# A pre-norm attention block and a feed-forward block in one kernel: the order of work changed at the start, at the change of batch, at the entrance of the feed-forward part and over its last product

## What is computed

```python
def attn(x, Wqkv, bqkv, Wo, bo):                    # one head, d = 256
    q, k, v = split(x @ Wqkv + bqkv, 3)
    a = softmax(q @ k.T / 16)
    return (a @ v) @ Wo + bo

def ffn(h, gate_w, up_w, down_w, fc1_w, fc2_w, expert_w, gamma, beta):
    top = sum(top_k(h @ gate_w, 2))                 # per row
    shared = relu(h @ up_w)**2 @ down_w             # 1024 -> 2048 -> 1024
    routed = ((h @ fc1_w) @ expert_w * top) @ fc2_w # 1024 -> 512 -> 512 -> 1024
    return norm(shared + routed) * gamma + beta

x = x + attn(norm(x), ...)
x = x + ffn(norm(x), ...)
```

## Time and profile before

| what | us |
|---|---|
| median of 3 runs | 2403.39 |
| lowest and highest of them | 2400.56, 2404.26 |
| the profiled execution's own time | 2403.08 |
| its span in the trace | 2401.2 |
| PE busy | 2320.8 (97% of the span) |
| DVE busy | 1748.3 (73%) |
| POOL busy | 1565.5 (65%) |
| ACT busy | 907.8 (38%) |

### The profile page before, as it was taken

How to read it: one execution, slowest core, us unless ns; L and a number is a source line. 1 busy time by engine, 2 the same in 40 slices (tenths; PEclk the granted TensorE clock), 3 DMA queues, 4 the chain that set the end, 5 groups by cost and what they waited for, 6 DMA issues and landing times.

```text
span 2401.2 us, 31321 instructions
## 1 busy us (share of the span) xinstructions
PE 2320.8 (97%) x11224; PEld 1937.2 (81%) x11224; DVE 1748.3 (73%) x2946; ACT 907.8 (38%) x1707; POOL 1565.5 (65%) x1180
## 2 busy tenths in 40 slices
PE   7999999999999899999999999999999999999996
PEld 5888889888988788878877887887787787788875
DVE  5889857876887544854689865479785368977868
ACT  4222233432434343444433443432344343344442
POOL 4466535664666776599557489846659974844584
PEclk8999999999999999999999999999999999999998
DMA  8899847778778633435345343535444533533452
GB/s 232 263 305 301 252 140 196 216 218 283 218 200 230 209 113 95 130 90 149 97 140 163 101 127 94 151 94 172 130 115 105 138 109 109 185 106 97 119 158 88
DMA packets 216090, 386.48 MB, mean 161 GB/s; under 512 B 19584, under 2 KB 95488, under 8 KB 215296
## 3 DMA queue, kind: packets, MB, share of 16 engines
q1 hardware_dynamic: 214784, 382.38, 54.1%
q10 hardware_dynamic: 1152, 2.10, 0.2%
HBM read 260.67 MB, written 90.18 MB: 146 GB/s over the span
## 4 chain that ended last, share of the span: by engine, by line
PE 55%; DVE 18%; POOL 13%; DMA 6%; issue 5%; SPq 2%; ACT 1%; DVEq 0%; POOLq 0%; ACTq 0%
PE ps L2199 18%; PE ps L2201 18%; PE ps L2200 18%; DVE pturn L1334 5%; POOL hq L2041 4%; DMA pland<-pturn 4%; POOL wr1l L1957 2%; POOL wr0l L1957 2%; POOL wr2l L1957 2%; SPq L638 1%; DVE x L1361 1%; DVE mx L1317 1%; DVE xi L1270 1%; DVE xr L1599 1%; DVE st L1368 1%
## 5 line engine op out<-in xcount | busy, mean ns | idle before, releaser
L1957 POOL TENSOR_TENSOR wr2l<-stf,wr2h 128x512 fp32r<-128x512 f32 x183 | 261.0, 1426 | 153.3 <-ACT wr2h L963 153.2
L1957 POOL TENSOR_TENSOR wr0l<-stf,wr0h 128x512 fp32r<-128x512 f32 x184 | 258.5, 1405 | 150.5 <-ACT wr0h L963 150.2
L1957 POOL TENSOR_TENSOR wr1l<-stf,wr1h 128x512 fp32r<-128x512 f32 x183 | 256.6, 1402 | 152.2 <-ACT wr1h L963 152.2
L963 ACT CAST wr1h<-stf 128x512 fp32r<-128x512 f32 x183 | 113.8, 622 | 310.1 <-PE ps L2201 268.4
L963 ACT CAST wr0h<-stf 128x512 fp32r<-128x512 f32 x184 | 114.5, 622 | 307.6 <-PE ps L2201 270.3
L963 ACT CAST wr2h<-stf 128x512 fp32r<-128x512 f32 x183 | 113.9, 622 | 303.6 <-PE ps L2201 255.8
L1957 POOL TENSOR_TENSOR pt<-pland,pt 128x512 fp32r<-128x512 f32 x120 | 153.0, 1311 | 69.6 <-ACT pt L942 69.6
L932 ACT ACTIVATE prob<-ps,nm 128x512 f32<-128x512 f32 x128 | 86.3, 688 | 251.7 <-DVE nm L1325 251.7
L1334 DVE STREAM_TRANSPOSE pturn<-prob 128x512 f32<-128x512 f32 x128 | 131.9, 1094 | 56.5 <-DMA pland<-pturn 51.1
L1212 DVE TENSOR_TENSOR hr1l<-hq,hr1h 128x512 fp32r<-128x512 f32 x78 | 98.2, 1259 | 85.4 <-ACT hr1h L986 85.1
L1212 DVE TENSOR_TENSOR hr0l<-hq,hr0h 128x512 fp32r<-128x512 f32 x78 | 91.5, 1173 | 89.5 <-ACT hr0h L986 89.5
(11 more groups left out here) (488 smaller groups left out, 7774.0 us busy)
## 6 DMA issues: line engine op xcount, KB each, us to landing
stf<-ups SPq DMA_DIRECT2D x160, 256.0 KB, 3.0
stf<-downs SPq DMA_DIRECT2D x160, 256.0 KB, 2.9
pland<-pturn SPq DMA_DIRECT2D x120, 256.0 KB, 4.7
stf<-in_upw_dram SPq DMA_DIRECT2D x120, 256.0 KB, 2.6
stf<-in_down_dram SPq DMA_DIRECT2D x88, 256.0 KB, 2.6
x<-in_x_dram SPq DMA_DIRECT2D x32, 512.0 KB, 6.5
x1d<-x SPq DMA_DIRECT2D x32, 512.0 KB, 5.6
xi<-in_x_dram SPq DMA_DIRECT2D x28, 512.0 KB, 9.4
```

The costliest lines, as they stand in the source:

```text
L963: eng.copy(hi, src).then_inc(*a_w.up(K))
L1957: eng.tensor_tensor(lo, src, hi.bitcast(F32), ALU.subtract).then_inc(*done)
```

## The change

**Start.** Three more stage buffers, and a table STG_BUF that says which piece goes into which. Two low parts (et 2, f2 2/0) go from DVE to POOL, et 3 from POOL to DVE behind the root, one piece (f2 2/1) is taken ahead of the variance. DVE norms 5 of 16 groups, not 4. ACT takes one more piece ahead of the norm, and interleaves E2's first two banks with the first two slab pieces.

**Change of batch.** In pair 7 DVE takes the turns of group 15 ahead of the moments of units 2 and 3 and of the root; SP issues group 15's shuffle and the key loads ahead of `store1(5)` and `qload(9)`; POOL's `norm2(5)` goes behind the split of group 14. In pair 8 `xadd(7)` goes first on POOL and `at_hi`/`at_low`(7,1) go earlier. In pair 9 PE runs output unit 0 of pair 7 ahead of the scores, not behind.

**Entrance of the feed-forward part.** POOL splits weights 0, 1 and 2 ahead of `xadd(15)` and `norm2(14)`.

**Last half block.** The order of the products becomes 1, 2, 6, 5, 3, 7, 4. The last product runs wholly by banks: all ten steps for bank 0, then for bank 1, 2, 3. Its weights and hidden rows are prepared earlier, with other buffers. The x rows of tiles 0 to 3 are loaded and beta added in the up half (steps 46 to 59), those of tiles 4 to 7 at down steps 0 to 11. Tiles 0 to 3 are finished during the last product, tiles 4 and 5, then 6 and 7, behind it, all on DVE.

The core of the diff:

```diff
-DOWN = [(1, 2, 6, 3, 7, 4, 5)] * 3 + [(1, 2, 6, 7, 4, 5, 3)]
+DOWN = [(1, 2, 6, 3, 7, 4, 5)] * 3 + [(1, 2, 6, 5, 3, 7, 4)]
...
-    late = [47, 48, 49, 51, 53, 54, 55, 57, 58, 59]
+    late = [38, 40, 42, 47, 48, 49, 50, 51, 57, 58]
...
+        STG_BUF = [0, 1, 2, 3, 4, 0, 1, 2, 3, 4, 0, 5, 6, 7, 1, 2, 3]
-        STG_DVE = [("et", 0), ("f2", 0, 0), ("f2", 0, 1), ("f2", 1, 1), ("et", 2), ("f2", 2, 0), ("f2", 2, 1)]
+        STG_DVE = [("et", 0), ("f2", 0, 0), ("f2", 0, 1), ("f2", 1, 1), ("f2", 2, 1), ("et", 3)]
...
-        for i, s in enumerate((41, 43, 45, 47, 49, 51, 53, 58, 59, 60)):
+        for i, s in enumerate((31, 33, 35, 37, 39, 41, 43, 45, 47, 49)):
... SyncE, attention
+                if C == 7:
+                    xload(C - 1)
+                    shuffle(odd)
+                    for kb in (2, 3):
+                        load_k(kb)
                 if C >= 2:
                     store1(C - 2)
-                xload(C - 1)
+                if C != 7:
+                    xload(C - 1)
...
-                if C < 15:
+                if C < 15 and C != 7:
                     shuffle(odd)
-                if C == 7:
-                    for kb in (2, 3):
-                        load_k(kb)
... SyncE, last block, up half
+                        if fin and s in (46, 48, 50, 52):
...
+                            load_x1(n, t, xrl[t])
... ScalarE, start
-            for k in STG[:11]:
+            for k in STG[:12]:
                 stage_hi(k)
...
-            for k in STG[11:13]:
-                stage_hi(k)
-            for j in range(2):
-                slab_hi(0, j)
+            stage_hi(STG[12])
+            slab_hi(0, 0)
+            e2_evac(0)
+            slab_hi(0, 1)
+            e2_evac(1)
             for k in STG[13:15]:
                 stage_hi(k)
-            for lt in range(2):
-                e2_evac(lt)
... VectorE, start
             aggr1(0, stats1(0, 8, 16), 8, 16)
+            low(stg_parts(("f2", 2, 1)), a_stg["f2", 2, 1], v_stg.up(("f2", 2, 1)))
             diff1(0)
-            for k in STG_DVE[4:]:
-                low(stg_parts(k), a_stg[k], v_stg.up(k))
             rstd1(0)
...
+            low(stg_parts(("et", 3)), a_stg["et", 3], v_stg.up(("et", 3)))
... VectorE, pair 7
                     for u in (2, 3):
                         residual(C - 2, u)
+                    turns(odd)
+                    at_low(C - 1, 0)
+                    for u in (2, 3):
                         moments(C - 2, u)
+                    at_low(C - 1, 1)
                     ln2(C - 2, *range(15))
-                    at_low(C - 1, 0)
-                    turns(odd)
-                    at_low(C - 1, 1)
... GpSimd, entrance and up half of the last block
-            w_low(0)
+            for k in range(3):
+                w_low(k)
             xadd(15)
             norm2(14, 0)
             norm2(14, 1)
-            w_low(1)
-            w_low(2)
...
+                        if fin and s in (50, 53, 56, 59):
+                            add_beta(n, (s - 50) // 3, xrl[(s - 50) // 3])
... TensorE
+                elif C == 9:
+                    wo_unit(C - 2, 0)
+                    scores(even)
+                    wo_unit(C - 2, 2)
+                    wo_unit(C - 2, 3)
...
-            for ts in ((0, 1), (2,), (3,)):
-                for s in range(63, 70):
-                    down_mm(NBK - 1, s, ts)
+            for t in range(4):
+                for s in range(60, 70):
+                    down_mm(NBK - 1, s, (t,))
```

More of the change, by code:

```diff
@@ L840, in _ @@
                             load_x1(n - 1, t + 2, xr[t % 2])
[L841 to L843 removed]
+                for s in range(60 if fin else 70):
+                    turnover(PER * n + 70 + s)
                     if not fin:
```

338 lines of the change are left out of this document (139 added, 199 removed).

## The result

| | us |
|---|---|
| before, median of 4 runs | 2403.23 (2400.56 to 2404.26) |
| changed, median of 4 runs | 2389.91 (2388.09 to 2395.01) |
| changed against before | 0.995, 95% interval 0.9931 to 0.9968 |
| forecast | 2378.0, range 2371 to 2388 |

A forecast was written before the change was run, and what follows sets the result against it. PE was busy 97%, so time could come only from its gaps, half-clock stretches and the work after its last matmul; -4.2 -0.6 -4.8 +0.5 -6.4 -9.5 = -25.0 against 2403.08 gave 2378, range 2371 to 2388.

The forecast's parts named there:

- Start, -4.2: Start: first projection 2.75 us earlier and its half-clock stretch gone, 1.45; bounds -1.5 and -6.
- Change of batch, -0.6: Pairs 7 to 9: wait at 538 goes, but store1(5) lands behind the keys and delays pv(7,0); bounds +1.5 and -3.5.
- Rival A: Change of batch: stores land with or before the keys, pv(7,0) about 3 us earlier, sum 2374; chance 0.15.
- Entrance, -4.8: Feed-forward entrance: 5.73 wait and 1.6 at half clock go, part given back, step 4 at 807.45; bounds -2.5 and -6.5.
- Last block, up half, +0.5: Last block's up half: eight beta additions on POOL cost little, using DVE's idle time; bounds 0 and +5.
- rival B: Up half: POOL's additions hold DVE, PE waits 2.8 and loses 1.7 or more; 5 us, 2382.5; chance 0.16.
- My worst case: Up half: all eight additions delay DVE in full, 10.4 us against 5.6 caught up; wait 2.8, stretch 1.7 or more.
- Down half, -6.4: Last block's down half: waits and 3.05 of half clock go, 7.2, less 0.8 at steps 49 and 50; bounds -3.5 and -7.2.
- End, -9.5: Behind PE's last matmul: only the last bank's work is left, 11.8 to 12.0 us for 21.5; bounds -7 and -10.5.
- Rival C: End: DVE comes late, its spare of 3 being an estimate; end gains only 5, sum 2382.7; chance 0.13.
- Rival D: Last product: PE starves for late hidden pieces and stays at 1.2 GHz, 2408; chance 0.02 of ending above 2408.2.

The follow-up runs named there:

- store_first: Changed kernel with SyncE issuing store1(5) ahead of the shuffle and the keys in pair 7; 2387.07 us, ratio 0.9951.
- beta_split: Changed kernel with beta additions of tiles 0 to 3 at down steps 50, 52, 54, 56, their loads at 4 to 7; 2385.84 us, ratio 0.9930.
- entrance_root: Changed kernel with low parts of weights 1 and 2 on VectorE behind pair 14's root, GpSimd doing norm2(14) before xadd(15); 2387.55 us, ratio 0.9956.

## Why the prediction was wrong, point by point

**Start, -4.2: right**, measured -4.0. The first projection follows E2 without a wait (at 38.9, not 41; the trace that I read had a slow start), and its stretch at half clock is gone. That the size fits is in part luck: against the trace that it was worked out from (47.1) the stage is 5.4 us shorter, and against the mean of the four old starts 4.0.

**Change of batch, -0.6: the mechanism was right, the size off by 1.8.** The wait at 538 vanished, the store landed behind the keys, the residual waited for it. The step that was mis-sized is the wait ahead of `pv(7,0)`, forecast as 7 and 7.8 to 9.1 in the nine traces of this order (8.05 in the one above). In their mean `pv(7,0)` starts 28.3 us behind the start of the stage, where the forecast has 27.2 (550.35 less 523.19 in the trace that I read): 1.1 of the 1.8. Another 0.3 is that trace itself, with 68.36 the longest of the four old ones here. A stretch at half clock stands behind the wait; the window over it, changed kernel:

```profile
544.30:551.10 6.80, 3.29 (x15) 3.29 (x16) 3.99 (x6) 0.00 (x0) 1.04 (x1) 0.50 1.02 419
```

PE's clock is at its 1.2 GHz level for 6.8 us, 3.5 of them idle. That is no further loss: in this stage the kernel before has 10.2 us at 1.2 GHz, with PE busy in nearly all of them. Rival A falls: the store issued behind the keys was waited for, and with the store ahead of them (store_first) the wait is 3 us shorter.

**Entrance, -4.8: wrong**, measured -0.8. The step that failed: "The wait of 5.73 ... goes ... Given back: weight 3's low part ... 1.3 late", with the norm and the store "at about 802.6, as today". I kept the norm at its time and asked only what stands ahead of it on POOL. But it waits for the root on DVE, and the root was held for 10 us by POOL's own unbroken row. The norm came 2.37 us late for it, and weight 3 was waited for 3.60 us and not 1.3. Weight 4's fetch came 2.1 us late behind the store and took 4.4 us to land and not 2.9, so step 4 starts at 811.17 and not 807.45; why the landing took longer is open. The row for the pause was there: in the earlier trace rows POOL stands still for 1.54 us ahead of the additions, and the change filled that. The hold of 10 us is not needed for the loss: in beta_split's trace the root went through by turns, the norm waited 1.10, and the stage is as long. entrance_root put a pause back and got 2.7 us of its stage mean (68.4 to 65.7 over three kernels). The remaining 1.3 of my 4.8 are a wait for weight 3, which stands behind the additions in that order (2.02 us at 805.64).

**Last block, up half, +0.5: wrong**, measured +6.9, and +1.9 in the first down steps, which I had at nothing. This is rival B, to which I gave 0.16, and even its price of 5 was too low. The step that failed: "But an addition that falls on DVE's idle time costs nothing, and the table has DVE busy 73%." In that stage it is 97%. My worst case there was 5. It let DVE recover 0.8 us in each step; but the trace shows POOL's additions and low parts merging into one row (2149.83 to 2160.54, no pause over 0.1), and the engines slow one another: POOL's low parts take 1.60 and 1.75 for 1.30. An overlap costs DVE less than the whole addition that rival B names, though: 1.49, 1.73 and 1.77 for 0.68 or 0.69 are 0.8 to 1.1 us each.

**Down half, -6.4: right**, measured -5.5, within the bounds. The trace that I read had the longest of the four old stages (74.4 against a mean of 73.4), which is the difference.

**End, -9.5: right in kind**, measured -11.0, a little past its bound of -10.5. From the last matmul's end to the last addition's it is 7.9 us (2382.67 to 2390.58) where I had 8.2 to 8.6, and the store landed 2.6 us behind and not 3.2. Rival C did not occur, but was near: the spare was 0.2 us. Rival D did not occur: the clock is 1.00 over the last product, where PE is busy 46.41 of 46.60 us:

```profile
2336.00:2382.60 46.60, 46.41 (x204) 37.85 (x202) 40.40 (x83) 12.31 (x20) 16.85 (x13) 1.00 0.23 84
```

Together: +0.2, +1.8, +4.0, +8.3, +0.9 and -1.5 against the forecast make the 13.7 us that the sum of stages is short.

## What to carry to other kernels

Where work moves onto GpSimd, look at what VectorE does in that very stage, in a window over it and not in the whole-span share, and count a pause of GpSimd as room that VectorE lives on: a change that fills the pause can stop a chain of tiny operations for as long as GpSimd's row is. Work that is moved off the critical end must find a stage with room on both engines: here five placings of eight additions were tried, and each gave something back.

Read a stage in several executions before a wait in it is priced: the one trace I had was 1.4 us above the mean at the start and 1 us above it in the down half, and put on the record two gains that were partly luck. The wait ahead of `pv(7,0)` was 3.00 in it, and 4.7 to 5.0 in the other three traces of the old order.
